# A vision tower on one core: the expert bias spread issued behind the first index table, two row copies made by ScalarE, one padding store issued in image 0's step

## What is computed

```python
def _level(x, idx, W, b, p, gp):
    t = x.reshape(Bsz, C, h, p, h, p).transpose(0, 2, 4, 3, 5, 1).reshape(Bsz, h * h, p * p * C)
    t = t[:, idx].reshape(Bsz, h * h // gp, gp * p * p * C)
    return t @ W.T + b
outs = [outs[0]] + [_interp_linear(o, n_tokens) for o in outs[1:]]
h = jnp.concatenate(outs, axis=-1) @ Wf.T + bf
h = h + attn(layernorm(h))          # 12 heads of 16
h = h + ffn(layernorm(h))           # x + sum of the two picked experts' gated outputs
```

## Time and profile before

| | us |
|---|---|
| median of 3 runs | 800.95 |
| lowest and highest of them | 797.98, 802.77 |
| the profiled execution's own time | 795.69 |
| its span | 794.0 |
| outside the span | 1.69 |
| TensorE busy | 698.3 (88%) |
| VectorE, ScalarE, GpSimd busy | 454.2, 367.1, 387.6 |

### The profile page before, as it was taken

The page is one execution under the profiler, slowest core; times in us unless marked ns, Lnnn a source line. Parts: engine busy times, 40 slices in busy tenths (PEclk is TensorE's granted clock), DMA queues, the critical chain, the costliest instruction groups (busy, mean ns, idle before and its releaser), DMA issues.

```text
span 794.0 us, 22662 instructions
## 1 busy us (share of the span) xinstructions
PE 698.3 (88%) x7845; PEld 602.2 (76%) x7845; DVE 454.2 (57%) x1318; ACT 367.1 (46%) x882; POOL 387.6 (49%) x599
## 2 busy tenths in 40 slices
PE   3207879999999999999988989999999999999995
PEld 3106756677777777777666878999999999998995
DVE  7102035678888888888877736434444445443448
ACT  1002225666666666666656333434443354433352
POOL 7760022356777777777757544333333333332422
PEclk9999999999999999999989999999999999999998
DMA  8629255434444444444415933566725741669659
GB/s 186 158 50 197 46 109 120 103 99 110 109 117 111 107 112 110 111 108 112 114 47 145 273 95 100 163 168 177 208 67 149 208 119 55 183 156 261 184 190 342
DMA packets 96715, 110.68 MB, mean 139 GB/s; under 512 B 18418, under 2 KB 84979, under 8 KB 96307
## 3 DMA queue, kind: packets, MB, share of 16 engines
q1 hardware_dynamic: 79122, 79.56, 39.0%
q0 software_dynamic: 11792, 27.18, 11.6%
q10 hardware_dynamic: 5712, 2.79, 2.1%
HBM read 142.13 MB, written 33.96 MB: 222 GB/s over the span
## 4 chain that ended last, share of the span: by engine, by line
issue 36%; PE 17%; POOL 16%; DVE 13%; another core or an unknown queue 6%; POOLq 4%; DMA 3%; SPq 3%; ACT 2%; DVEq 0%; ACTq 0%
POOL pixels L761 5%; PE BK L877 4%; POOL slot_rows L1951 3%; PE BK L1011 3%; POOLq L760 3%; DVE negmax L1622 2%; POOL pair_rows L751 2%; PE BK L970 2%; POOL rs L1900 2%; PE BK L990 2%; POOL hr L1940 2%; PE BK L931 1%; PE BK L1022 1%; DVE hr L745 1%
## 5 line engine op out<-in xcount | busy, mean ns | idle before, releaser
L539 ACT ACTIVATE pixels<-BK,shared 128x128 f32<-128x128 f32 x474 | 131.1, 375 | 194.3 <-PE BK L496 147.1
L496 PE MATMUL BK<-pixels,shared 64*128 64x128 f32 x2844 | 174.9, 273 | 3.5 <-issue 2.6
L496 PEld LDWEIGHTS BK<-pixels,shared 64*128 64x128 f32 x2844 | 169.5, 188 | 6.9 <-issue 5.5
L751 POOL DMA_INDIRECT pair_rows<-pixels x79 | 78.3, 992 | 197.1 <-DVE pixels L714 172.5
L515 PE MATMUL BK<-shared,pixels 64*128 64x192 f32 x1752 | 160.3, 328 | 2.5 <-DVE pixels L714 1.3
L515 PEld LDWEIGHTS BK<-shared,pixels 64*128 64x128 f32 x1752 | 142.4, 187 | 4.4 <-issue 4.3
L1622 DVE TENSOR_REDUCE negmax<-BK 128x6 f32<-128x1536 f32 x64 | 112.4, 1757 | 25.7 <-PE BK L990 23.2
L1368 ACT ACTIVATE shared<-BK 128x1536 f32<-128x1536 f32 x64 | 92.8, 1449 | 10.2 <-PE BK L1011 9.0
L1951 POOL DMA_INDIRECT slot_rows<-xr,adr x64 | 64.9, 1014 | 36.7 <-issue 14.6
L700 DVE TENSOR_TENSOR pixels<-pixels 128x1 int32<-128x1 f32 x60 | 9.6, 160 | 106.6 <-PE BK L482 106.6
L990 PE MATMUL BK<-shared 96*128 96x256 bf16 x384 | 53.9, 277 | 3.8 <-DVE negmax L1622 2.3
(11 more groups left out here) (245 smaller groups left out, 1164.4 us busy)
## 6 DMA issues: line engine op xcount, KB each, us to landing
shared<-ew SPq DMA_DIRECT2D x150, 288.0 KB
shared<-ew SPq DMA_DIRECT2D x75, 576.0 KB
shared<-qk_parts SPq DMA_DIRECT2D x112, 96.0 KB
shared<-expert_biases SPq DMA_DIRECT2D x75, 99.0 KB
pixels<-slot_rows POOLq DMA_DIRECT2D x64, 104.0 KB
qk_parts<-shared SPq DMA_DIRECT2D x32, 192.0 KB, 2.0
shared<-qk_parts SPq DMA_DIRECT2D x16, 288.0 KB
shared<-pair_rows SPq DMA_DIRECT2D x12, 384.0 KB, 4.2
```

Source lines behind the costliest of these rows:

```text
L496: last = nc.tensor.matmul(hidden(t)[h * HC + c], w1h[w][rows, (k + h) % NK, c * P:(c + 1) * P], xtT[p][rows, k, :], start=(c == 0 and k == ...
L539: last = nc.scalar.activation(hT[p][:, c * P:(c + 1) * P], hidden(t)[c], ACT.Gelu, bias=bias[w][:, c:c + 1])
L751: nc.gpsimd.indirect_dma_start(pair_d, bass.IndirectOffsetOnAxis(t_dst[:, t:t + 1], 0), ysum[t % NB][:, :], None).then_inc(s[f"m_sc{t % NB ...
```

## The change

Three steps of the prologue are placed elsewhere, with the same data and the same sizes.

- The bias spread is issued by ScalarE as its first instruction, when the first index table (`ld_idx2`) has landed, in place of behind L1313.
- ScalarE makes the copies into `g1t` and `hrow[0:X0]` in place of VectorE, in `copies()` behind the issue of the first biases and ahead of `x1Ts`. The semaphores are `act_g1` and `act_w0`.
- The padding store from `padt` leaves the prologue of GpSimd. It is issued in step 0, between `f_qk3(1, 1)` and `a_nm(0, 0)`, and waits for image 0's queries and keys (`ld_qk0` at `N_QK`). The store from `padt2` stays.

```diff
@@ names of the semaphores
-                 "pe_wT act_wT pe_wf act_wf dve_wf dve_g1 dve_b ...
+                 "pe_wT act_wT pe_wf act_wf dve_wf act_g1 act_w0 dve_b ...
@@ sync
-            sp.wait_ge(s["dve_g1"], 1)
+            sp.wait_ge(s["act_g1"], 1)
             sp.dma_start(hrow[X0:X0 + T2, :, :], o2_d.rearrange("(b t) e -> t b e", t=T2)).then_inc(s["ld_o2"], 16)
@@ tensor, level2
-                pe.wait_ge(s["dve_g1"], 1)
+                pe.wait_ge(s["act_g1"], 1)
@@ tensor, level1
-                pe.wait_ge(s["dve_wf"], 2)
+                pe.wait_ge(s["act_w0"], 1)
@@ scalar, copies
             def copies():
+                act.wait_ge(s["ld_idx2"], 16)
+                nc.scalar.dma_start(bias_d[:, :, FC:FC + E], eb2.unsqueeze(1).to_broadcast([NE, P, E])) \
+                    .then_inc(s["st_bias"], 16)
                 act.wait_ge(s["pe_wT"], 1)
...
                 act.wait_ge(s["act_wf"], 2)
                 nc.scalar.dma_start(bias_d[:, :, 0:FC].rearrange("e p c -> p e c"), b1T[:, :, :]).then_inc(s["st_bias"], 16)
-                nc.scalar.dma_start(bias_d[:, :, FC:FC + E], eb2.unsqueeze(1).to_broadcast([NE, P, E])) \
-                    .then_inc(s["st_bias"], 16)
+                act.wait_ge(s["ld_g1"], 16)
+                nc.scalar.activation(g1t[:, :, :].rearrange("t b (g c) -> t b g c", c=C1),
+                                     g1[:, :, :].rearrange("t g (b c) -> t b g c", c=C1), ACT.Copy).then_inc(s["act_g1"], 1)
+                act.wait_ge(s["dve_wf"], 1)
+                act.wait_ge(s["act_g1"], 1)
+                nc.scalar.activation(hrow[0:X0, :, :], w0f[:, :].unsqueeze(1).to_broadcast([X0, B, E]), ACT.Copy) \
+                    .then_inc(s["act_w0"], 1)
                 act.wait_ge(s["pe_x1T_"], 1)
@@ vector
-            dve.wait_ge(s["ld_g1"], 16)
-            nc.vector.tensor_copy(g1t[:, :, :].rearrange("t b (g c) -> t b g c", c=C1),
-                                  g1[:, :, :].rearrange("t g (b c) -> t b g c", c=C1)).then_inc(s["dve_g1"], 1)
-            dve.wait_ge(s["dve_wf"], 1)
-            dve.wait_ge(s["dve_g1"], 1)
-            nc.vector.tensor_copy(hrow[0:X0, :, :], w0f[:, :].unsqueeze(1).to_broadcast([X0, B, E])) \
-                .then_inc(s["dve_wf"], 1)
@@ gpsimd
             pool.wait_ge(s["dve_init"], 5)
-            nc.gpsimd.dma_start(slot_d[0:NE * SEG, :].rearrange("(e s) c -> e s c", e=NE)[:, 0:P, :]
-                                .rearrange("e (b r) c -> e b (r c)", r=PR),
-                                padt[:, :, :].rearrange("p r c -> p (r c)")).then_inc(s["st_id0"], 16)
             nc.gpsimd.dma_start(slot_d[NE * SEG:NE * SEG + P * PR, :].rearrange("(p r) c -> p (r c)", r=PR),
                                 padt2[:, :, :].rearrange("p r c -> p (r c)")).then_inc(s["st_id1"], 16)
+
+            def padding_rows():
+                pool.wait_ge(s["ld_qk0"], N_QK)
+                nc.gpsimd.dma_start(slot_d[0:NE * SEG, :].rearrange("(e s) c -> e s c", e=NE)[:, 0:P, :]
+                                    .rearrange("e (b r) c -> e b (r c)", r=PR),
+                                    padt[:, :, :].rearrange("p r c -> p (r c)")).then_inc(s["st_id0"], 16)
@@ gpsimd, step
                 if on(1):
                     f_qk3(i + 1, 1, s["act_k2"], s["pool_k3"])
+                if isinstance(i, int) and i == 0:
+                    padding_rows()
                 if on(-4):
```

2 lines of the change are left out of this document (1 added, 1 removed).

## The result

| | before | after |
|---|---|---|
| median, us (4 runs each, same chip) | 800.1 (797.98 to 802.77) | 807.37 (805.96 to 810.45) |
| the profiled execution's own time | 795.69 | 805.96 |
| its span | 794.0 | 804.3 |
| TensorE busy | 698.3 (88%) | 703.6 (87%) |

The ratio of the runs is 1.0094, with an interval of 1.0049 to 1.0139: the change makes the kernel 0.9% slower. The medians are 7.3 us apart, the profiled executions 10.3. Of each kernel one execution was profiled, and the runs of one kernel lie up to 10 us apart, so the places in the traces are sure to about a microsecond only where several kernels agree.

The account below looks back on a forecast made before the run. The prediction took the prologue's stall, signals held until 62.24 us while GpSimd works on DMAs without pause, as the bound. +3.3 - 2.8 + 1.5 = +2.0 us on 800.95 gave 803.0, own range 799.5 to 806.5, with rivals 797.0 to 808.5.

Parts of the forecast that it names:

- the moved store is paid in full: Rival, image 0's step: store delays maxima and image 1's loads, +5.0 us there, +5.5 in all, 806.5 us; chance 0.17.
- Part 1: Prologue, bias spread at the head: costs 0, the stall covers the later fold; removes the 1.05 us gap before image 0.
- Part 2: Prologue, copies on ScalarE: 2.70 us copy, TensorE waits 4.3 us; with the early spread +3.3 us (2.2 to 4.4).
- Part 3: Prologue, one store fewer behind the gathers: stall ends at 59.4, -2.8 us (bounds 0.6 to 4.8 earlier).
- gathers alone set the stall: Rival, prologue: the 5.4 us tail isn't the stores' work, only 0.6 us goes; +4.2, 805.2 us; chance 0.17.
- Part 4: Image 0's step, moved store: GpSimd's time delays the maxima, store shares DMA with image 1's loads; +1.5 us (0 to +4).
- The sum: Whole kernel: +3.3 - 2.8 + 1.5 = +2.0 us, image 0's shift moving the end one for one; 803.0 us.
- the long stall breaks up: Rival, prologue: signals pass before GpSimd finishes, image 0 starts up to 30 us earlier; 771 to 795 us; chance 0.08.

Follow-up runs that it names:

- a3_spread_back: The changed kernel with the bias spread put back behind the first biases; 806.54 us, 1.0124 of the kernel before.
- a2_copies_back: The changed kernel with both row copies back on VectorE; 800.14 us, 1.0064 of the kernel before.
- b_copies: The kernel before with only the two row copies moved to ScalarE; 802.52 us, 1.0081 of the kernel before.
- r_after: The changed kernel itself, run again beside the kernels that do one part alone; 804.12 us, 1.0103 of the kernel before.
- a1_store_back: The changed kernel with the padding store from `padt` back behind the gathers; 798.02 us, 1.0034 of the kernel before.
- b_store: The kernel before with only the padding store moved, to the change's place in image 0's step; 800.36 us, 1.0069 of the kernel before.
- h1_one_pause: The kernel before with GpSimd waiting for the fold's signal ahead of its eighth level-0 gather; 774.23 us, 0.9723 of the kernel before.
- m1_own_pause: The kernel before with GpSimd waiting ahead of its eighth level-0 gather for its own first seven gathers only; 779.49 us, 0.9786.
- b_store_late: The kernel before with only the padding store moved, in image 0's step behind the second maxima; 799.19 us, 1.0058 of the kernel before.
- h4_copies_pause: The kernel before with both row copies on ScalarE and GpSimd waiting for the fold ahead of its eighth level-0 gather; 786.10 us, 0.9869.

## Why the prediction was off

The forecast was +2.0 us with a likeliest result within half a per cent; the result is +7.3 us in the medians. It lies in the range, beside the rival *the moved store is paid in full*, but that is in part luck: the forecast's own range ended at 806.5, and parts 3 and 4 were both off to the slow side, by 2.5 and 7.6 us. The +10.3 us of the profiled executions would have left the range, which ended 7.6 above the median that it was built on. The forecast's own range was also added up too narrowly. By the bounds as they stand it is -2.6 (2.2 - 4.8 + 0) to +7.8 (4.4 - 0.6 + 4), 798.4 to 808.8, not 799.5 to 806.5. By its steps:

- **Part 1, cost 0: right.** The fold's last instruction ran 9.3 us later (TensorE's L877 at 32.52 against 23.20) and nobody waited; a3_spread_back gains nothing by undoing it. The 1.05 us gap ahead of image 0 went, as forecast, and a2_copies_back shows it to be this part's; with the copies on ScalarE it goes without this part as well (a3_spread_back). A gain that the forecast didn't name came in its place: without this part ScalarE's copy starts later, behind the issue of the spread, by 0.5 us in a3_spread_back and 1.7 in b_copies.
- **Part 2, +3.3 together with part 1: right.** The copy took 2.75 us for 2.70, TensorE waited 4.28 for 4.3. Image 0 was late by 3.67, and would have been by 4.0 without the 0.35 of part 3; the 0.7 above the forecast are those of L922 (6.25 us for 5.55), which r_after doesn't have. a1_store_back shows 3.75 at image 0 and a time of 0.4 to 5.0 us above before, so whether part of such a shift is made good behind isn't shown.
- **Part 3, -2.8: this step failed.** It took the 5.4 us between the stores' records and the signal for the stores' own work. Two stores or one, the signal comes at the same time within the scatter of the profiles (61.90 to 62.24 in three kernels with two, 61.73 to 62.30 in six with one). The rival *gathers alone set the stall* had it right, at 0.17. The argument against that rival, 1.2 us behind the scatters and 5.4 here, was sound as a difference, but it had a third explanation that I didn't look for: how long the row of DMAs had been, four scatters there and 42 gathers here.
- **Part 4, +1.5: the largest error, by the size of one term.** It was 9.1 us in image 0's step (8.2 in b_store), for a price of 1.5 and an upper bound of 4. I had priced GpSimd's time, which turned out free: the maxima weren't delayed at all. I had priced the loads of queries and keys, and no wait for them shows, though one could hide behind the wait for `nmT`. The transfer that was late is one that I didn't list, the 9 KB of `nmT`, issued 5 us behind the store and needed at once. The rival had the mechanism (a small transfer beside a bulk one, 6.5 us more by the earlier trace rows; the wait was 6.14) and then let the loads' slack take 1.5 of it and knew nothing of the clock: the other 3.0 of the 9.1 us stand beside the matmuls at the lower clock behind the wait, 1.7 of them in the 8 records of L970 alone.
- **The sum.** With the measured terms it is +3.7 at image 0 (parts 1 to 3) + 9.1 = +12.8 at the first L1022 (147.46 against 134.65). At TensorE's last L496 it is +9.8 (789.8 against 780.0). It looks as if 3 us were made good on the way, but that isn't shown: from the first L1022 to the end of the span the fourteen profiles take 656.8 to 664.0 us without an order, and r_after, the same kernel, has +11.7 at L1022 and +10.8 in the span. In the runs the change costs 0.9 to 1.0%, 7 to 8 us; of the gap to 10.3, some is in the profiled execution of before, which at 795.69 lies 2.3 us below the fastest of its four runs. That a shift of image 0 shifts the end one for one is thus neither shown nor refuted to better than 3 to 5 us.

The rival *the long stall breaks up*, at 0.08, didn't happen in this change, and its reason against it ("nothing in the trace speaks for it") stands. But h1_one_pause gives 774.2 us, inside the 771 to 795 that it named, by another lever.

## What to carry to other kernels

Before moving a bulk store into a busy stretch, list every small DMA that an engine waits for in the next 15 us, not only the large ones near it: here 9 KB behind 1664 KB cost 6 us of waiting and 3 of clock, while the issuing engine lost nothing. Where an engine starts long behind the instruction that it waits for, and another engine issues DMAs without a break all that time, try a pause in that row before moving any work: one wait gave 2.8%, where three moves of work cost 0.9%. And measure a change again once the stall in front of it is gone: the copies that cost 3 us (a2_copies_back) to 6 (b_copies) with the stall cost some 12 without it (0.9869 against 0.9723).

## What the runs showed of the hardware

- Signals come late while GpSimd issues indirect DMAs back to back, by up to 38 us for one of TensorE to ScalarE and VectorE (before), though the DMA engines are only 0.14 busy. The held one passes 1.2 us (4 DMAs in the row) to 6.3 to 7.0 us (42) behind the end of the row, and a pause of 3 to 4 us in the row lets it through (h1_one_pause, m1_own_pause). Some pass inside a row, after 6.57 us in m1_own_pause.
- VectorE's wait for its own result takes 1.24 us beside gathers that have run for 22 us (before), and is gone at the end of a pause, where the same instructions start 0.19 us apart (h1_one_pause).
- TensorE's own stream creeps in the same stretches with "issue" as the reason: in h1_one_pause the last matmuls of level 1 came one or two in 0.7 us or more from 55.3 to 61.6 us.
- A transfer of 9 KB issued by SyncE 1 us behind a store of 1664 KB of GpSimd was in use 9.1 us later (b_store_late). In after, SyncE's issue of three loads beside that store took 4.31 us instead of 1.42, and ScalarE's issue of the bias spread took 2.28 and 2.42 us behind two such stores and 0.98 behind one (b_copies and before, a3_spread_back).
- A copy of VectorE from SBUF to SBUF, 3072 numbers on 64 partitions, lengthened a gather of GpSimd from 0.95 to 2.37 us (h1_one_pause); ScalarE's copy of the same took 2.75 us instead of 1.74 and left the gathers alone (h4_copies_pause).
